# A windowed attention block: queries and keys made as 128 channels plus 64 by halves, and a new order of SP's transfers

## The reference

```python
f = _ln(x.transpose(0, 2, 3, 1), g1, b1)
f = jnp.roll(f, (-3, -3), axis=(1, 2)); win = _window_partition(f)     # 49 tokens a window
qkv = win @ w_qkv + b_qkv                                              # 96 -> 288
attn = softmax(einsum('bhid,bhjd->bhij', q, k) * scale + mask)
out = einsum('bhij,bhjd->bihd', attn, v) @ w_proj + b_proj
f = x + roll(window_reverse(out), (3, 3))
m = gelu(_ln(f, g2, b2) @ w_fc1 + b_fc1) @ w_fc2 + b_fc2               # 96 -> 192 -> 96
return f + m
```

## Time and profile before

| | us |
|---|---|
| median of 3 executions | 3043.04 |
| lowest, highest | 3038.63, 4634.42 |
| the profiled execution | 3049.62 |
| its span in the profile | 3047.8 |
| TensorE busy in the span | 2874.4 |
| VectorE busy | 2422.0 |
| ScalarE busy | 2040.3 |
| GpSimd busy | 1773.8 |

### The profile page before, as it was taken

How to read it: one execution, slowest core, us unless ns; L and a number is a source line. 1 busy time by engine, 2 the same in 40 slices (tenths; PEclk the granted TensorE clock), 3 DMA queues, 4 the chain that set the end, 5 groups by cost and what they waited for, 6 DMA issues and landing times.

```text
span 3047.8 us, 141611 instructions
## 1 busy us (share of the span) xinstructions
PE 2874.4 (94%) x54852; PEld 2400.5 (79%) x54852; DVE 2422.0 (79%) x7206; ACT 2040.3 (67%) x3208; POOL 1773.8 (58%) x2088
## 2 busy tenths in 40 slices
PE   1799999999999999999999999999999999999997
PEld 0578888788887888788887888878888788888876
DVE  5778888788887888778887888878888788888885
ACT  0467767677676777667766767767767677767774
POOL 2555666556655656555565666655565565566655
PEclk9899999999999999999999999999999999999999
DMA  1444444444444444444444444444444444444441
GB/s 30 107 120 124 126 129 122 120 128 121 125 124 112 126 127 121 120 119 123 126 124 116 127 127 122 127 114 123 126 123 121 116 128 123 125 125 123 129 112 42
DMA packets 414933, 359.65 MB, mean 118 GB/s; under 512 B 63645, under 2 KB 414175, under 8 KB 414202
## 3 DMA queue, kind: packets, MB, share of 16 engines
q1 hardware_dynamic: 414218, 350.03, 44.1%
HBM read 193.28 MB, written 154.14 MB: 114 GB/s over the span
## 4 chain that ended last, share of the span: by engine, by line
PE 88%; ACT 5%; issue 4%; DVE 2%; POOL 1%; SPq 0%; DMA 0%; DVEq 0%; POOLq 0%; ACTq 0%
PE psum L473 18%; PE psum L457 10%; PE psum L394 8%; PE psum L441 8%; PE psum L499 7%; PE psum L514 6%; PE psum L559 5%; PE psum L586 5%; PE psum L587 5%; PE psum L401 5%; ACT probs L646 4%; PE psum L405 3%; PE psum L549 3%; PE psum L422 2%; PE psum L538 1%
## 5 line engine op out<-in xcount | busy, mean ns | idle before, releaser
L646 ACT ACTIVATE probs<-psum 113x784 f32<-113x784 f32 x768 | 632.4, 823 | 670.1 <-PE psum L457 666.8
L758 DVE TENSOR_REDUCE nmax<-psum 113x16 f32<-113x784 f32 x768 | 745.4, 971 | 174.9 <-PE psum L441 174.6
L355 POOL TENSOR_SCALAR ve<-mv 98x8 f32<-98x8 f32 x264 | 64.3, 244 | 1150.7 <-DVE mv L787 1111.9
L473 PE MATMUL psum<-vbd,probs 128*49 128x18 f32 x24576 | 649.0, 198 | 5.8 <-issue 5.3
L473 PEld LDWEIGHTS psum<-vbd,probs 128*49 128x49 f32 x24576 | 638.9, 127 | 6.9 <-issue 6.3
L457 PE MATMUL psum<-qbd,kst 128*49 128x196 f16 x6144 | 410.8, 252 | 43.6 <-DVE xfl L793 21.5
L362 POOL TENSOR_TENSOR rs<-ve,half 98x8 f32<-98x8 f32 x264 | 440.2, 1667 | 0.0
L367 POOL TENSOR_TENSOR xn<-xn,rs 98x768 f32<-98x768 f32 x264 | 387.9, 1469 | 74.5 <-POOL rs L362 74.3
L782 DVE BATCH_NORM_STATS2 st<-tok 98x6 f32<-98x96 f32 x2112 | 363.7, 246 | 84.8 <-ACT tok L653 71.3
L441 PE MATMUL psum<-kbd,qst 128*49 128x196 f16 x6144 | 403.1, 251 | 7.6 <-DVE nmax L758 4.6
L358 POOL TENSOR_TENSOR xn<-tok,mv 98x768 f32<-98x768 f32 x264 | 389.9, 1477 | 1.7 <-POOL ve L355 1.7
(11 more groups left out here) (90 smaller groups left out, 5673.3 us busy)
## 6 DMA issues: line engine op xcount, KB each, us to landing
stack_pages<-nat SPq DMA_DIRECT2D x256, 294.0 KB, 3.0
kst<-stack_pages SPq DMA_DIRECT2D x256, 220.5 KB
qbd<-stack_pages SPq DMA_DIRECT2D x1024, 55.1 KB
stack_pages<-nat SPq DMA_DIRECT2D x256, 147.0 KB, 2.0
xr<-in_x_dram SPq DMA_DIRECT2D x224, 147.0 KB, 3.4
out_dram<-yr SPq DMA_DIRECT2D x224, 147.0 KB, 2.2
qst<-stack_pages SPq DMA_DIRECT2D x256, 73.5 KB
kbd<-stack_pages SPq DMA_DIRECT2D x1024, 18.4 KB
```

What stands on the lines that cost most here:

```text
L473: last = nc.tensor.matmul(dst[:, :, h, :], probs[:, b.c % 2, h // 4, p, h % 4 * L:(h % 4 + 1) * L], vbd[:, b.c % 4, p * NH + h, :, :], sta ...
L646: nc.scalar.activation(probs[0:PR, b.c % 2, u, :, :].rearrange("j (g q) k -> j g (q k)", g=2), psum[0:PR, B:B + 2, 0:2 * CH], ACT.Exp).the ...
L758: nc.vector.tensor_reduce(dst, psum[0:PR, A:A + 2, 0:2 * CH].rearrange("i g (q h j) -> i g q h j", q=2, j=L), axis=AX.X, op=ALU.max, negat ...
```

## The change

Queries and keys together are 192 channels, the same as FC1's hidden width, and are now made in the same form: 128 channels of all tokens (96 queries and the first 32 keys), then the other 64 keys of either half of the tokens. `nat` has that shape too, and both conversions work on 128 rows of 588 elements instead of 96 of 784. The page in HBM keeps its layout, so that it is written in more pieces: the high parts in four transfers instead of one, both parts in three instead of one; the reads are unchanged.

In TensorE's order `most` and `rest` are separate. In the odd step both bands' full products of FC1 come first and then both bands' half-width ones; `back` waits for the first gelu only; `project` stands between the full and the half-width products of queries and keys. In the even step the rest follows the full products at once. In SP's order the high parts of band t+3 come first, then the load, the maxima of t+1, the key blocks, the stores, both parts of t+3, and the stacks of t+2.

```diff
--- before.py
+++ after.py
@@ -126,7 +126,7 @@
         st, mv = sb("st", [PT, 2, 2 * PAIRS, 6]), sb("mv", [PT, 2, 2 * PAIRS, 2])
         ve, rs = sb("ve", [PT, 2, 2 * PAIRS]), sb("rs", [PT, 2, 2 * PAIRS])
         xfh, xfl = sb("xfh", [FULL, 4, 2, TOK], F16), sb("xfl", [FULL, 4, 2, TOK], F16)
-        nat = sb("nat", [C, 4, 4, TOK], F16)
+        nat = sb("nat", [FULL, 4, 2, 3, PART], F16)
         kst = sb("kst", [FULL, 3, QUADS, TOK], F16)
         qbd = sb("qbd", [FULL, 2, NH, TOK], F16)
         kbd = sb("kbd", [FULL, 2, NH, TOK], F16)
@@ -146,11 +146,9 @@
         A, B, D, O_BANK, V_BANK, O_HALF = 0, 2, 6, 4, 5, 256
 
         side = C * 3 * TOK
-        stack_pages = nc.dram_tensor("stack_pages", [4, 2 * (side + 3 * TOK)], F16, kind="Internal").ap()
-        q_stack = [stack_pages[n, 0:side].rearrange("(c m t) -> c m t", m=3, t=TOK) for n in range(4)]
-        k_stack = [stack_pages[n, TOK + side:TOK + 2 * side].rearrange("(c m t) -> c m t", m=3, t=TOK) for n in range(4)]
-        both_parts = [stack_pages[n, TOK:TOK + 2 * side].rearrange("(s c m t) -> c s m t", s=2, m=3, t=TOK)[:, :, 0:2, :] for n in range(4)]
-        high_parts = [stack_pages[n].rearrange("(s r) -> s r", s=2)[:, 0:side].rearrange("s (c m t) -> c s m t", m=3, t=TOK)[:, :, 0, :] for n in range(4)]
+        stack_pages = nc.dram_tensor("stack_pages", [4, 2 * side + 3 * TOK], F16, kind="Internal").ap()
+        pages = [stack_pages[n].rearrange("(c m t) -> c m t", m=3, t=TOK) for n in range(4)]
+        q_stack, k_stack = ([stack_pages[n, at:at + side].rearrange("(c m t) -> c m t", m=3, t=TOK) for n in range(4)] for at in (0, TOK + side))
 
         consts_in, filled, rows_one, vbd_zero, vbd_ones = sem("consts_in"), sem("filled"), sem("rows_one"), sem("vbd_zero"), sem("vbd_ones")
         psum_clear, weights_wide, weights_high, weights_set = sem("psum_clear"), sem("weights_wide"), sem("weights_high"), sem("weights_set")
@@ -164,6 +162,7 @@
         max_in = [sem(f"max_in{n}") for n in range(2)]
         y_out = [sem(f"y_out{n}") for n in range(8)]
         STACK_IN, KEY_IN = 5 * 16, 5 * 16
+        HIGH_OUT, NAT_OUT = 4 * 16, 3 * 16
         X_IN = [16] * 7 + [2 * 16]
 
         passed = sem("passed")
@@ -260,7 +259,7 @@
                 n = b.c % 2
                 wait(sp, s_made, b.count(QUADS, -QUADS))
                 alone(sp)
-                sp.wait_ge(high_out[b.c % 4], b.used(4, 16))
+                sp.wait_ge(high_out[b.c % 4], b.used(4, HIGH_OUT))
                 alone(sp)
                 sp.dma_start(qst[0:QUAD, masked_slot(b), :, :], q_stack[b.c % 4].rearrange("(c a) m t -> m a c t", c=QUADS)[0]).then_inc(key_in[n], 16)
                 for h in range(4):
@@ -271,7 +270,7 @@
                 n = b.c % 4
                 wait(sp, p_made, b.count(QUADS, -QUADS))
                 alone(sp)
-                sp.wait_ge(nat_out[n], b.used(4, 16))
+                sp.wait_ge(nat_out[n], b.used(4, NAT_OUT))
                 alone(sp)
                 sp.dma_start(kst[0:C, masked_slot(b), :, :], k_stack[n].rearrange("(c a) m t -> (a m) c t", c=QUADS)).then_inc(stack_in[n], 16)
                 for h in range(4):
@@ -284,16 +283,25 @@
                 alone(sp)
                 sp.dma_start(qbd[MAXROW:MAXROW + 1, n, :, :], mrow[:, n, :]).then_inc(max_in[n], 16)
 
-            def save_parts(b):
+            def save_high(b):
                 n = b.c % 4
                 wait(sp, stack_in[n], b.step(-4).used(4, STACK_IN))
                 alone(sp)
                 sp.wait_ge(qk_high, b.count(1, 1))
                 alone(sp)
-                sp.dma_start(high_parts[n], nat[:, n, 0:4:2, :]).then_inc(high_out[n], 16)
+                most = nat[:, n, 0, 0:2, :].rearrange("c s t -> c (s t)")
+                sp.dma_start(pages[n][0:C, 0, :], most[0:C]).then_inc(high_out[n], 16)
+                sp.dma_start(pages[n][C + 1:FULL + 1, 0, :], most[C:FULL]).then_inc(high_out[n], 16)
+                for s in range(2):
+                    sp.dma_start(pages[n][FULL + 1:2 * C + 1, 0, s * PART:(s + 1) * PART], nat[REST * s:REST * (s + 1), n, 0, 2, :]).then_inc(high_out[n], 16)
+
+            def save_both(b):
+                n = b.c % 4
                 sp.wait_ge(qk_low, b.count(1, 1))
                 alone(sp)
-                sp.dma_start(both_parts[n], nat[:, n, :, :].rearrange("c (s m) t -> c s m t", s=2)).then_inc(nat_out[n], 16)
+                sp.dma_start(pages[n][0:FULL, 1:3, :], nat[:, n, :, 0:2, :].rearrange("c m s t -> c m (s t)")).then_inc(nat_out[n], 16)
+                for s in range(2):
+                    sp.dma_start(pages[n][FULL:2 * C, 1:3, s * PART:(s + 1) * PART], nat[REST * s:REST * (s + 1), n, :, 2, :]).then_inc(nat_out[n], 16)
 
             def store_y(b):
                 sp.wait_ge(y_made, b.count(1, 1))
@@ -302,14 +310,14 @@
                     sp.dma_start(out[b.image(), :, row:row + rows, :], yr[:, b.c % 2, at:at + rows, :]).then_inc(y_out[b.c % 8], 16)
 
             def step(t):
-                for offset, stage in ((LOAD, load_x), (KEYS, key_blocks)):
+                for offset, stage in ((QK - 1, save_high), (LOAD, load_x), (SCORE - 1, maxima), (KEYS, key_blocks)):
                     if has(t.step(offset)):
                         stage(t.step(offset))
                 if odd(t):
                     for offset in STORE:
                         if has(t.step(offset)):
                             store_y(t.step(offset))
-                for offset, stage in ((STACK, stacks), (SCORE, maxima), (QK, save_parts)):
+                for offset, stage in ((QK - 1, save_both), (STACK, stacks)):
                     if has(t.step(offset)):
                         stage(t.step(offset))
 
@@ -388,19 +396,20 @@
             pe.wait_ge(weights_set, 1)
             pe.wait_ge(vbd_ones, 1)
 
-            def three(dst, high, low, b, kind):
-
-                for n, (weights, tokens) in enumerate(((high, xfh), (high, xfl), (low, xfh))):
-                    last = nc.tensor.matmul(dst, weights, tokens[:, b.c % 4, kind, :], start=n == 0, stop=n == 2)
+            def products(high, low):
+
+                return enumerate(((high, xfh), (high, xfl), (low, xfh)))
+
+            def most(bank, high, low, b, kind):
+
+                for n, (weights, tokens) in products(high, low):
+                    last = nc.tensor.matmul(three_parts(bank)[:, 0:2, :], weights[:, 0:FULL], tokens[:, b.c % 4, kind, :].rearrange("c (s t) -> c s t", s=2),
+                                            start=n == 0, stop=n == 2)
                 return last
 
-            def most_and_rest(bank, high, low, b, kind):
-
-                products = ((high, xfh), (high, xfl), (low, xfh))
-                for n, (weights, tokens) in enumerate(products):
-                    nc.tensor.matmul(three_parts(bank)[:, 0:2, :], weights[:, 0:FULL], tokens[:, b.c % 4, kind, :].rearrange("c (s t) -> c s t", s=2),
-                                     start=n == 0, stop=n == 2)
-                for n, (weights, tokens) in enumerate(products):
+            def rest(bank, high, low, b, kind):
+
+                for n, (weights, tokens) in products(high, low):
                     for s in range(2):
                         last = nc.tensor.matmul(psum[REST * s:REST * (s + 1), bank + 1, 0:PART], weights[:, FULL:FULL + REST], tokens[:, b.c % 4, kind, s * PART:(s + 1) * PART],
                                                 start=n == 0, stop=n == 2)
@@ -505,7 +514,7 @@
                     return
                 pe.wait_ge(normed, b.count(1, 1))
                 if odd(t):
-                    wait(pe, gelu_done, t.step(HIDDEN[1]).count(1, 1)) if has(t.step(HIDDEN[1])) else None
+                    wait(pe, gelu_done, t.step(HIDDEN[0]).count(1, 1)) if has(t.step(HIDDEN[0])) else None
                 if has(t.step(PROB)):
                     pe.wait_ge(exp_done, t.step(PROB).count(QUADS, QUADS))
                 wait(pe, n_low, b.count(1))
@@ -524,9 +533,12 @@
                     pe.wait_ge(tokens_in, t.step(TURN).count(1, 1))
                 elif has(t.step(SCORE)):
                     pe.wait_ge(s_maxed, t.step(SCORE).count(QUADS, QUADS))
-                for m in range(2):
-                    last = three(psum[0:C, at + m, 0:TOK], wh[:, m * C:(m + 1) * C], wl[:, m * C:(m + 1) * C], b, 0)
-                last.then_inc(qk_made, 1)
+                most(at, wh, wl, b, 0)
+
+            def queries_keys_rest(t):
+                b = t.step(QK)
+                if has(b):
+                    rest(D if odd(t) else A, wh, wl, b, 0).then_inc(qk_made, 1)
 
             def max_transpose(t):
                 b = t.step(SCORE)
@@ -568,8 +580,12 @@
                         pe.wait_ge(exp_done, t.step(PROB).count(QUADS, QUADS))
                 elif has(t.step(SCORE)):
                     pe.wait_ge(s_maxed, t.step(SCORE).count(QUADS, QUADS))
-                last = most_and_rest((B, A)[n], w1h, w1l, b, 1)
-                last.then_inc(fc1_made, 1)
```

(19 more changed lines are left out.)

## The result

The changed kernel takes 3238.1 us (median of 4, 3230.1 to 3247.6) against 3042.1: ratio 1.065, 95% interval 1.061 to 1.069. Forecast: 3000, range 2975 to 3060.

What follows compares the result with a forecast made beforehand. TensorE, 94% busy, was taken as the bound, with a few waits on its chain; 0.30 + 0.04 = 0.34 us a pair times 127 pairs, 43 us, gave 3000 us, range 2975 to 3060.

Steps and rivals of the forecast that it cites:

- SP's queue: SP's transfers: ten more a pair raise it from 16.0 to 20.2 to 23.2 us, 20.7 taken, against a 22.3 us pair.
- The wait for high_out: SP's queue ahead of the key blocks: a new wait for its own high parts, 0.7 to 2.7 us a pair.
- Rival 1: SP's queue becomes the bound once the change adds over 6.3 us a pair: slower, 3140 us; chance 0.13.
- scores idle for key blocks: On TensorE, sign of being wrong: scores wait for key blocks, which were expected to cost nothing while SP stays below a pair.
- high parts landing in 3 us or more: SP's transfers, sign of being wrong: high parts land that late, where 2.0 us after issue was the known landing.
- The FC1 step: FC1, odd step: grouping both bands saves about 0.20 us of changing width, but the second band starts at 0.70, so no gain.
- the maximum that eats TensorE's 0.20: VectorE's third maximum, ending at 0.62, holds the second band's full products, so TensorE's 0.20 us saving is lost.
- `back` earlier by 0.26: Odd step: `back` waits for the first gelu alone and starts at 2.55 instead of 2.81, a 0.26 us gain.
- the table load as next: ScalarE's table load ends last before the exponential, at 6.94 instead of 7.24; 0.18 us of TensorE's gain is spent waiting.
- The pair of 21.9: TensorE: an undisturbed odd and even step takes about 21.9 us between first FC1 products, against 22.22 before.
- Queries and keys, even step: TensorE: the queries and keys products cost 0.96 us instead of 1.00, saving 0.04 us a pair.
- the lumps: Mean pair above the undisturbed 22.22 us: 0.42 us, coming in some pairs only, assumed to stay.

Runs made afterwards that it cites:

- seven saves by channels: The kernel before with 7 saves a step instead of 2, cut by channels so every piece keeps its 784 bytes: ratio 1.005 (1.002 to 1.008).
- four full-width saves: The changed kernel with 4 full-width saves a step instead of 7, half-width parts left out, so attention uses wrong queries and keys: 0.979, 2975 us.
- FC1 alone: The kernel before with only the FC1 part of the change, `back` waiting for the first gelu: ratio 0.986, 2992 us.

## Why the prediction was wrong

- The step that failed is in "SP's queue": "Four key-block transfers are issued in 1.34 us, with the gaps 0.35 each: ten more are 3.5 us, and 4.5 if they stall as the dearer ones do". I priced writes of several shapes by reads of 8 rows. Measured: seven saves sum to 0.32 + 0.43 + 0.48 + 0.60 + 0.39 + 0.63 + 0.61 = 3.46 us by their medians (the two L296 and the two L304 each by their place), against 0.64 for two: 5.6 us more a pair, about 0.5 of gaps, and the rest of the 7.9 (some 1.8) in long single issues: about 1.0 of it in the saves themselves, whose means sum to 4.03 us where the two of before have 0.70, the rest in the transfers around them. The trace of before had the warning, had I used it: nothing in it issues saves one behind the other, and the nearest other small write, the row of maxima, takes 0.52.
- The wait for high_out, 0.7 to 2.7 a pair in my sum, was 23 us in the whole run, 0.2 a pair: the high parts land 1.9 us after issue and SP is busy until then. The total, 20.2 to 23.2, was under 23.9 at both ends.
- Rival 1 is what happened: its place, SP's queue; its point, 6.3 us more a pair (6.5 more in the seven saves by channels cost 0.5%); its make-up only in part, for 2.7 of its 7.2 us were that wait, and the measured 7.9 are issue and gaps. Its price, 3140, was 98 us short, and 0.13 was too little for an end at 23.2 over a decision point at 22.3. The range stopped below its price. The range's upper end should have been its time.
- Of the signs of being wrong, scores idle for key blocks came true (167 us); high parts landing in 3 us or more did not.
- The FC1 step, the maximum that eats TensorE's 0.20, `back` earlier by 0.26 (0.29 measured), and the table load as next: right within 0.03 us each, in the run with four full-width saves. The pair of 21.9 was 21.96 there.
- The 0.04 us saved in "Queries and keys, even step" was wrong by sign. The products take the forecast 0.96, but `project` behind half-width products takes 0.74 to the next start (1376.78 to 1377.52), where it took 0.65 (1363.82 to 1364.47 of before). I had counted the change back inside the 0.38. So the pair lost 0.05 there. TensorE's timeline of before, the same place behind the 96-column products:

```profile
1363.82 0.82 PE L559 MATMUL psum<-oT,wp 128*96 128x392 f32 x2
1364.47 0.49 PE L586 MATMUL psum<-hid,w 128*96 128x196 f32 x2
```

- I kept the lumps (0.42 us a pair) constant. With FC1 alone the mean pair fell by 0.46 (22.63 to 22.17) and the undisturbed by 0.29. The forecast's 3000 is a ratio of 0.986; FC1 alone, for which 0.989 was expected, reached 0.986 by the shrunk lumps, and the four saves 0.979. Why the lumps shrank stays open.
- So the TensorE half of the reckoning held, even step apart, but the changed kernel shows none of its gain: SP's pair, 23.9 us, was longer than TensorE's.
- Narrow pieces cost nothing that these runs can show: issue and time stay when they are made wide, and the high parts in 392-byte pieces land 1.9 us after issue, where the one large save of before took 2.0. (The row of maxima, which I called no later than 147 KB, lands 2.1 us after issue, 0.1 later.)

## What to carry to other kernels

Count a queue as an engine: sum its issue times and gaps over a period, and compare with the period before adding transfers; slack in waits is soon spent, and just under it nothing shows. Take means, since a few long issues stand behind a small median. Price a transfer by one of its own kind, direction, rows and neighbours, and where the trace has none, take the dearest row for the upper end. A layout that saves matmul time is paid for in transfers, and if its consumer is bound by something else (here a table load) there is nothing to set against it.

## What the hardware showed unexpectedly

- SP's issue of a save from `nat` goes by its rows and its place behind another, not by its bytes or width: 96 rows 0.32 us in the first place, 0.43 to 0.45 in the second, at 392 or 784 bytes a piece; 128 rows 0.39; 32 rows in the second place 0.43, but 0.60 behind 64 rows; 64 rows 0.48 to 0.63.
- The longest single issue of SP is 2.0 us or more in every trace. Issues over 1 us are 3.6% of SP's transfers before and 6.4% after (160 to 2960 us), so that medians alone undercount a queue.
- GpSimd took 0.60 us to issue a stack read where SP takes 0.37.
